# A pipelined one-core kernel: four small moves in its queues, and logits turned by whole rows

## The reference

```
x = x + gla_and_ffn(layernorm(x))    # gated linear attention, 16 heads, then a gelu feed-forward of 512, in float32
x = x + moe(layernorm(x))            # 8 experts of 256x256, the best 2 by softmax of router logits
x = x + recurrence(layernorm(x))     # h = tanh(xB + h A^T) over the tokens, 16 states, then C and W_out
x = x + moe(layernorm(x))            # the same experts again
```

## Time and profile before

| | us |
|---|---|
| median of 3 runs | 1692.7 (1692.68, 1697.66, 1692.70) |
| the profiled execution | 1692.37 |
| its span, first to last instruction | 1690.6 |
| busy: PE / PEld / DVE / ACT / POOL | 1587.4 / 1331.8 / 1271.7 / 1035.1 / 824.5 |
| mean granted TensorE clock | 0.972 of full |

### The profile page before, as it was taken

The page is one execution under the profiler, slowest core; times in us unless marked ns, Lnnn a source line. Parts: engine busy times, 40 slices in busy tenths (PEclk is TensorE's granted clock), DMA queues, the critical chain, the costliest instruction groups (busy, mean ns, idle before and its releaser), DMA issues.

```text
span 1690.6 us, 51149 instructions
## 1 busy us (share of the span) xinstructions
PE 1587.4 (94%) x16584; PEld 1331.8 (79%) x16584; DVE 1271.7 (75%) x4557; ACT 1035.1 (61%) x3852; POOL 824.5 (49%) x1293
## 2 busy tenths in 40 slices
PE   4688999999999999999999999999999999998866
PEld 3577888888888888888888888888888888887654
DVE  4566778887888778887887787878878877776544
ACT  4655666666766666666666666666666667655431
POOL 3554455554555455545554554455545545543211
PEclk8798999999999999999999999999999999999978
DMA  5211111111111111111111111111111111110000
GB/s 150 86 56 46 52 58 56 43 40 43 43 56 56 56 52 42 35 50 45 56 56 56 48 44 31 50 50 56 56 56 44 37 44 44 52 51 8 7 6 13
DMA packets 117121, 81.48 MB, mean 48 GB/s; under 512 B 41888, under 2 KB 108096, under 8 KB 116928
## 3 DMA queue, kind: packets, MB, share of 16 engines
q1 hardware_dynamic: 116080, 80.10, 15.5%
q10 hardware_dynamic: 976, 0.54, 0.1%
HBM read 47.06 MB, written 33.55 MB: 48 GB/s over the span
## 4 chain that ended last, share of the span: by engine, by line
PE 60%; DMA 15%; DVE 8%; SPq 7%; issue 5%; ACT 2%; POOL 1%; ACTq 0%; DVEq 0%; POOLq 0%
PE ps L1253 48%; DMA xag<-in_x 11%; DMA arow<-att 5%; SPq L314 3%; SPq L338 3%; PE ps L1259 2%; DVE acc L892 2%; PE ps L1270 2%; PE ps L1299 2%; PE ps L1440 2%; PE ps L1319 2%; PE ps L1310 2%; DVE att L949 1%; DVE hs L860 1%; POOL orstd L517 1%
## 5 line engine op out<-in xcount | busy, mean ns | idle before, releaser
L1253 PE MATMUL ps<-we,yT 128*128 128x512 f32 x3072 | 832.1, 411 | 5.3 <-DVE sub L915 0.8
L1253 PEld LDWEIGHTS ps<-we,yT 128*128 128x128 f32 x3072 | 540.4, 190 | 108.9 <-DVE sub L915 8.3
L566 ACT ACTIVATE h_lead<-ps 48x8 fp32r<-48x8 f32 x1024 | 172.1, 168 | 460.0 <-PE ps L1270 448.9
L860 DVE SCALAR_TENSOR_TENSOR hs<-ps,cst,h_lead 48x8 fp32r<-48x8 f32 x1024 | 224.0, 219 | 222.8 <-ACT ps L567 217.3
L1270 PEld LDWEIGHTS ps<-hs,aT 128*128 128x128 f32 x1024 | 195.4, 191 | 106.0 <-DVE hs L860 70.9
L1270 PE MATMUL ps<-hs,aT 128*128 128x8 f32 x1024 | 210.1, 205 | 40.1 <-DVE hs L860 39.5
L892 DVE SCALAR_TENSOR_TENSOR stage<-ps,coef,stage 128x256 f32<-128x256 f32 x384 | 183.0, 476 | 13.9 <-POOL stage L432 5.5
L892 DVE SCALAR_TENSOR_TENSOR acc<-ps,coef,acc 128x256 f32<-128x256 f32 x384 | 182.1, 474 | 10.8 <-POOL acc L432 4.2
L517 POOL TENSOR_TENSOR orstd<-omean,mhalf 128x32 f32<-128x32 f32 x32 | 174.8, 5462 | 0.2
L567 ACT ACTIVATE ps<-ps 48x8 f32<-48x8 f32 x1024 | 163.2, 159 | 0.0
L430 POOL TENSOR_TENSOR part<-part 128x256 f32<-128x256 f32 x64 | 47.2, 737 | 205.1 <-ACT part L584 202.7
(11 more groups left out here) (185 smaller groups left out, 3200.2 us busy)
## 6 DMA issues: line engine op xcount, KB each, us to landing
arow<-att SPq DMA_DIRECT2D x32, 512.0 KB, 2.8
atx<-arow SPq DMA_DIRECT2D x128, 128.0 KB, 2.8
vrow<-vtok SPq DMA_DIRECT2D x32, 256.0 KB, 2.1
vx<-vrow SPq DMA_DIRECT2D x128, 64.0 KB, 2.0
out<-stage SPq DMA_DIRECT2D x64, 128.0 KB
xin<-in_x SPq DMA_DIRECT2D x62, 128.0 KB
xag<-in_x SPq DMA_DIRECT2D x62, 128.0 KB
stage<-in_experts SPq DMA_DIRECT2D x1, 2048.0 KB, 10.2
```

What stands on the lines that cost most here:

```text
L566: a.activation(h_lead[:], ps[0:NB, BANK["RB"], k * B:(k + 1) * B], ACT.Tanh)
L860: v.scalar_tensor_tensor(hs[0:NB, :, k], h_whole, keeps_rest, h_lead[:].bitcast(F32), ALU.mult, ALU.subtract).then_inc(sem("rnn_h"), 1)
L1253: ins = t.matmul(dst, left(lp, c), right(rp, c), start=(n == 0), stop=(n == 3 * chunks - 1))
```

## The change

Six edits. On GpSimd the sum res += xmid moves from ahead of elast and rstd_f to behind both. On ACT the Exp of m2 moves behind scaled_second(m1, 1) and state_of(18). On DVE rest(hTs) and split_state(10) go ahead of the second half of y1, in the order hTs, split 10, y1; and split_state(16) goes ahead of rest(h2Ts). On PE logits_by_token turns all 128 rows of m.y in place of 16 (the rows below the logits hold the mixture's normed input), into 128 columns for each tile; top_two reads the first 16 columns of each.

```
 GpSimd
-                if live(it, 3):
-                    pool.wait_ge(sem("xmid"), c3)
-                    pool.wait_ge(sem("res"), c3)
-                    g.tensor_tensor(res[:], res[:], xmid[:], ALU.add).then_inc(sem("res_mid"), 1)
                 if live(it, 2):
                     pool.wait_ge(sem("dec"), c2)
                     g.tensor_tensor(elast[:], ...).then_inc(sem("elast"), 1)
...
                     pool.wait_ge(sem("mv_f"), target)
                     rstd(mv_f, rf, "f", c3)
+                if live(it, 3):
+                    pool.wait_ge(sem("xmid"), c3)
+                    pool.wait_ge(sem("res"), c3)
+                    g.tensor_tensor(res[:], res[:], xmid[:], ALU.add).then_inc(sem("res_mid"), 1)
 ACT
                     state_of(17, c6)
+                if live(it, 5):
+                    scaled_second(m1, 1, BANK["G1_4"])
+                if live(it, 6):
+                    state_of(18, c6)
                 if live(it, 7):
                     act.wait_ge(sem("sub2"), c7)
                     a.activation(m2.p[:], m2.sub[:], ACT.Exp).then_inc(sem("p2"), 1)
-                if live(it, 5):
-                    scaled_second(m1, 1, BANK["G1_4"])
-                if live(it, 6):
-                    state_of(18, c6)
 DVE
-                pieces = ps[:, bank, TOK:TOK + TILES * ROUTED].rearrange("p (i s e) -> p i e s", i=TILES, e=E)
+                pieces = ps[:, bank, TOK:2 * TOK].rearrange("p (i w) -> p i w", i=TILES)[:, :, 0:ROUTED].rearrange("p i (s e) -> p i e s", e=E)
...
                     combine(m2, 7, 1, BANK["G2_7"], c7)
-                if live(it, 3):
-                    normed(y1, xmid, mv_f[:, :, 0], rf[:, 1, :], 1).then_inc(sem("y1"), 1)
-                if live(it, 5):
-                    split_state(10, c5)
                 if live(it, 1):
                     dve.wait_ge(sem("hT0"), c1)
                     rest(hTs, by_chunk("Y0"), "hTs")
...
+                if live(it, 5):
+                    split_state(10, c5)
+                if live(it, 3):
+                    normed(y1, xmid, mv_f[:, :, 0], rf[:, 1, :], 1).then_inc(sem("y1"), 1)
...
+                if live(it, 5):
+                    split_state(16, c5)
                 if live(it, 3):
                     dve.wait_ge(sem("h2T0"), c3)
                     rest(h2Ts, by_chunk("Y1"), "h2Ts")
-                if live(it, 5):
-                    split_state(16, c5)
 PE
-                    ins = t.transpose(ps[:, bank, TOK + i * ROUTED:TOK + (i + 1) * ROUTED], m.y[0:ROUTED, 0, i * P:(i + 1) * P], ident[0:ROUTED, 0:ROUTED])
+                    ins = t.transpose(ps[:, bank, TOK + i * P:TOK + (i + 1) * P], m.y[:, 0, i * P:(i + 1) * P], ident)
```

More of the change, by code:

```diff
@@ L742, in body @@
                     state_of(17, c6)
-                if live(it, 7):
-                    act.wait_ge(sem("sub2"), c7)
-                    a.activation(m2.p[:], m2.sub[:], ACT.Exp).then_inc(sem("p2"), 1)
                 if live(it, 5):
@@ L749, in body @@
                     state_of(18, c6)
+                if live(it, 7):
+                    act.wait_ge(sem("sub2"), c7)
+                    a.activation(m2.p[:], m2.sub[:], ACT.Exp).then_inc(sem("p2"), 1)
                 if live(it, 2):
```

## The result

| | before | after |
|---|---|---|
| median of the runs | 1692.84 us (1689.95 to 1697.66, 6 runs) | 1707.74 us (1704.43 to 1712.59, 6 runs) |
| profiled execution | 1692.4 us, span 1690.6 | 1706.5 us, span 1704.5 |

What follows compares the result with a forecast made beforehand. Middle rounds were taken as bound by att to xag's landing, xhat to sub, then PE to the next att (48.4 to 48.8 us). Middle 0, edges -1.0: profiled 1691.4, median 0.3 above, 1691.7 us; own range 1688 to 1695, wider 1682 to 1698.

Steps and rivals of the forecast that it cites:

- (b): GpSimd: rstd of the middle norm ahead of res += xmid; y1's first half about 0.35 us earlier, cost 0.
- (c): DVE: y1's second half behind hTs and step 10's split; hs 10 about 0.1 us later, covered by xhat's wait, 0.
- (a): DVE: step 16's split ahead of h2Ts; step 17 loses its 0.51 us wait, sub unmoved, gain 0 mid-run.
- (d): ACT: Exp of the m2 scores behind the second scaling and state 18; Exp at most 0.3 us later, worth 0.
- (e): PE: whole-row turns of the logits, twice a round; a pair +0.04 us, in no term of the round.
- The three terms: A middle round: att to xag's landing 15.0 to 15.4, xhat to sub 2.92, PE to next att 30.5 us.
- Rival A: PE is the bound, its step 17 wait worth full length: 13.8 us gained, 1678 us; full or half 13%.
- Rival B: xag's landing shifts with other DVE and GpSimd traffic; half of xhat's wait gone, 8 us: 1683 us; 7%.
- Rival C: DVE late at step 10's split behind hTs; 0.24 us beyond xhat's wait in 27 rounds, 6.5 us: 1698; 11%.
- The edges: Some 7 filling and draining rounds not held by xag, gaining 0.15 us each: -1.0 us.

Runs made afterwards that it cites:

- sum early: The changed kernel with GpSimd's res += xmid back ahead of elast and rstd_f, the other five edits kept: 1696.3 us, ratio 1.0024.
- (a) alone: The kernel before with only step 16's split moved ahead of h2Ts on DVE: 1692.9 us, ratio 1.0017.

## Why the prediction was wrong

The failed step is (b), in its words: "The addition then runs from about 1012.5 to 1013.8 ... nobody waits. Cost 0." The time of the addition was right (it starts with y1), and so was the list of its readers. What I did not ask was what runs on DVE in just these 1.3 us, though (c) says it: "y1's first half from 1012.53". It measured 1.37 us for the 0.41 I carried. Over 24 rounds, with what (a) makes of it, that is the 13.8 us; without it (sum early) the rest of the change is at 1.0024.

The trace of before showed it. Two of its y1, in the filling, took 1.35 and 1.37 us beside the same sum. In the middle rounds it is other instructions: grel, a tensor_scalar of 128 x 256 like y1, beside a GpSimd addition of 0.74 us,

```profile
L963 DVE TENSOR_SCALAR grel<-grel x32: 275/772/783, 18.7 to 1474.4; 128x256 f32<-128x256 f32 x32
```

and DVE's two<-p, 128 x 2, with 142 ns at least and 673 at most in the view of its line. The timelines of GpSimd and DVE have the reason beside it:

```profile
1027.02 0.74 POOL L432 TENSOR_TENSOR acc<-mx_in,part 128x256 f32<-128x256 f32 x1
```

```profile
1027.11 0.67 DVE L922 TENSOR_TENSOR two<-p 128x2 f32<-128x2 f32 x1
```

Two columns in 0.67 us, ending at 1027.78, with GpSimd's sum ending at 1027.76. I read only the rows of the moved instructions, not the spread of a group. By the Trainium skill (SBUF — State Buffer, SBUF: two separate sides and Who interferes with whom) DVE and GpSimd share one port pair as an exclusive lock, and a DVE instruction with two SBUF inputs or in a two-port mode waits until a GpSimd instruction that started first has ended. The trace agrees with it for the sum: 1.37 us, ending 0.16 us behind it. Whether y1 runs in such a mode, no run shows. I did not weigh that rule, and it speaks against this change.

- (a) "sub stays at xhat + 2.92", "ACT has nothing late for it": held alone (a round of 48.45), failed beside (b), where the tanh is 0.32 us late and xhat to sub 3.29. ACT had been read in a round where every step was on time.
- (b) Also partly right: y1 starts earlier; wait for rf 9.8 us in all in the kernel after, in 31 rounds, 0.27 in the round shown. I had said near 0.1.
- (c) "hs 10 comes about 0.1 us later": 0.28 alone, free as said.
- (d) No run has it by itself; with the sum early it is in 1.0024.
- (e) I gave the pair +0.04. With the turns alone, step 10, right behind the pair of m1, starts at att + 6.20 in place of 6.38, and the pair of m2 0.10 us earlier: cheaper, not dearer, though each turn is longer (0.27 us in place of 0.23 and 0.21). By the Trainium skill (TensorEngine Tiling (Array Packing), Key Properties) a change of the tiling mode drains TensorE, so that was to be; the trace agrees in sign. It is worth nothing while xag is what a round waits for, as said: step 12 starts at att + 9.60 with either.
- The three terms are three consecutive pieces of a round, so that they add up to it proves nothing. What the runs do show is that the third is 30.5 us in every kernel here, and that a round changed only by what (b), (a) or the load made of the other two. xhat's wait, their cover, was sized wrong: the mean of 0.63 us holds one wait of 5.3, and in the middle rounds it is 0.41.
- Rival A (PE the bound) is out: (a) alone moves no round, and 1.1% came with PE's work unchanged. To relieve the engine of the highest occupancy first, as the Trainium skill (Perfetto Trace Analysis, Identifying the Most-Contended Engine) has it, would lead astray here, 99.2% busy or not; the trace disagrees.
- Rival B (the landing moves) did not happen: 15.08 us behind att, before 15.02.
- Rival C had the sign, the place where it decides ("beyond xhat's 0.63 us wait") and a price of 1698, but the wrong cause: I looked for late inputs (ACT's copy, the moments), and all of them were on time. Its 0.24 us a round is near the 0.21 measured on att to xhat by luck: 0.87 of lateness beyond 0.63 of cover, where it was 0.6 (att + 15.27 in place of the 14.65 at which DVE comes to xhat when no load holds it) beyond 0.4; the other 0.39 is (a)'s. My 11% for it rested on inputs alone.
- The edges: I had -1.0. In the profiled executions the filling is -4.8 and the stretch behind the three last rounds +2.7. As the filling differs by as much between kernels with the same order, this neither bears the -1.0 out nor refutes it.

Open: the 3.6 us of the sum-early kernel and the 2 to 3 us of (a) alone. The median middle round has none of them, so most is at the ends of the run, where single executions vary by as much; no run here places them. From the last att to the end the profiled executions with (a) take 196.7 to 200.6 us (six kernels), those without it 195.6 to 199.0 (seven). That (a) costs them in both is likely, not shown.

## What to carry to other kernels

When an instruction moves on GpSimd, list what runs on DVE during its new interval, and look in the trace for the same forms beside a GpSimd instruction. Here tensor_scalar on SBUF and the forms with two tiles in SBUF were held: price those as ending when GpSimd's ends, and then follow what is late next. A group in which the maximum is several times the minimum at one shape is the sign that this already happens; look at the other engine at that moment. Price moves together: a reordering that is free by itself (step 16's split) was paid for once another edit had eaten its slack. And where a round waits on one load, the order within that load's queue is the first thing to try: here it gained 1.1%, where the six edits lost 0.9%.

## What was not expected of the hardware

- Which DVE instructions are held by a GpSimd sum: tensor_scalar from SBUF (0.41 to 1.37 us), tensor_tensor of two small SBUF tiles (0.16 to 0.67), scalar_tensor_tensor with both in SBUF (to 1.51). Not held: a combine (0.47) and hTs (0.67), with one source in PSUM; and, with a single source in SBUF, the statistics of 128 x 256 (0.40 to 0.43) and the search for the largest values in lm (0.15 to 0.17 beside the sum in the run in which GpSimd waits for y1).
- GpSimd's power for the roots does not hold DVE. In the kernel before, with a 5.46 us span on GpSimd:

```profile
1027.72 5.46 POOL L517 TENSOR_TENSOR orstd<-omean,mhalf 128x32 f32<-128x32 f32 x1
```

```profile
1028.94 0.43 DVE L1188 SCALAR_TENSOR_TENSOR glog<-zb,ge 128x256 f32<-128x256 f32 x1 [0.72 <-ACT ge L760]
...
1030.99 0.40 DVE L883 TENSOR_SCALAR xhat<-xag,nrm 128x256 f32<-128x256 f32 x1
...
1032.74 0.41 DVE L1216 TENSOR_TENSOR grel<-gcum 128x256 f32<-128x256 f32 x1
```

  DVE's instructions of 128 x 256 from SBUF take 0.43, 0.40 and 0.41 inside it. The second is of y1's own form, and 32 of its kind there take 0.39 to 0.40. The Trainium skill (SBUF — State Buffer, SBUF: two separate sides) has the lock held for the whole instruction; for this operation the trace disagrees.
- Splitting GpSimd's sum in two frees DVE in between: y1 0.82 us in place of 1.37, and the ratio 1.001 in place of 1.009 for one instruction more.
